# Attention: query slots of two rounds filled, and the first queries transposed, in the second layer's input stage; transposed keys kept in four banks

## What is computed

```python
h = _rmsnorm(x, attn_norm_w)
q = (h @ w_q).reshape(b, l, N_HEADS, HEAD_DIM)        # 16 heads of 16
k = (h @ w_k).reshape(b, l, N_KV_HEADS, HEAD_DIM)     # 4 key heads, each shared by 4 query heads
v = (h @ w_v).reshape(b, l, N_KV_HEADS, HEAD_DIM)
q = _apply_rope(q, cos, sin); k = _apply_rope(k, cos, sin)
logits = jnp.einsum('bqhd,bkhd->bhqk', q, k) * scale
attn = jax.nn.softmax(jnp.where(causal, logits, -inf), axis=-1)
ao = jnp.einsum('bhqk,bkhd->bqhd', attn, v)
```

## Time and profile before

| | us |
|---|---|
| median of 3 runs (lowest to highest) | 1553.54 (1552.95 to 1556.1) |
| span of the profiled execution | 1551.7 |
| input stage: first instruction, end of the last | 1259.48, 1309.46 |
| attention: first instruction, end of the last | 1309.98, 1426.76 |
| experts: first instruction | 1427.19 |
| PE busy / DVE busy / ACT busy / POOL busy over the span | 1401.1 / 1046.9 / 865.6 / 534.3 |

### The profile page before, as it was taken

One profiled execution on the slowest core, in us unless ns is written; L12 is line 12 of the kernel. 1 busy time (PEld: TensorE's weight loads), 2 busy tenths in 40 slices (PEclk: granted clock), 3 DMA queues, 4 the chain that ended last, 5 costly groups with the idle time before them and its releaser, 6 DMA issues. The chain is left out here.

```text
span 1551.7 us, 35674 instructions
## 1 busy us (share of the span) xinstructions
PE 1401.1 (90%) x13996; PEld 1045.2 (67%) x13996; DVE 1046.9 (67%) x2132; ACT 865.6 (56%) x1740; POOL 534.3 (34%) x562
## 2 busy tenths in 40 slices
PE   4569999999999999999999999999899977998998
PEld 3335767777776777777677777777578754555855
DVE  4887686877868687786858778686735544773344
ACT  5555656666666665666666666666355316676210
POOL 1872332342323233233323323333335446541100
PEclk9678999999999999999999999999989988999999
DMA  5112020201202021020102102110311130002100
GB/s 168 37 49 59 9 39 16 67 22 20 41 14 38 16 67 29 13 46 21 27 16 66 29 13 45 23 25 21 91 36 44 41 89 1 1 1 52 31 14 14
DMA packets 142486, 56.39 MB, mean 36 GB/s; under 512 B 109776, under 2 KB 134992, under 8 KB 142064
## 3 DMA queue, kind: packets, MB, share of 16 engines
q1 hardware_dynamic: 133424, 48.20, 13.4%
q10 hardware_dynamic: 8896, 5.91, 1.2%
HBM read 37.11 MB, written 16.97 MB: 35 GB/s over the span
## 5 line engine op out<-in xcount | busy, mean ns | idle before, releaser
L1153 POOL TENSOR_TENSOR og<-og,sz 128x256 f32<-128x256 f32 x128 | 93.3, 729 | 518.8 <-DVE og L1096 300.9
L690 PE MATMUL banks<-wz,xT 128*128 128x256 f32 x512 | 129.2, 397 | 13.8 <-DVE yacc L1116 13.8
L943 DVE SCALAR_TENSOR_TENSOR Yv<-banks,cwall,Yv 128x511 f32<-128x511 f32 (+2 forms) x192 | 130.3, 740 | 7.5 <-ACT Yv L783 7.4
L542 PE MATMUL banks<-wv,xT 128*128 128x512 f32 x256 | 121.5, 619 | 11.1 <-DVE Yv L943 9.6
L761 PE MATMUL banks<-wo,oT 128*128 128x256 f32 x512 | 123.8, 385 | 0.0
L542 PE MATMUL banks<-wqk,xT 128*128 128x512 f32 x256 | 121.7, 610 | 0.2 <-DVE Yk L943 0.2
L690 PEld LDWEIGHTS banks<-wz,xT 128*128 128x128 f32 x512 | 96.3, 196 | 36.6 <-issue 23.9
L930 ACT ACTIVATE junk<-og 128x512 f32<-128x512 f32 x64 | 40.6, 634 | 121.1 <-POOL og L1153 121.1
L1160 POOL TENSOR_TENSOR rn<-ss,c_half 128x4 f32<-128x4 f32 x64 | 64.5, 1007 | 122.0 <-DVE ss L1110 122.0
L761 PEld LDWEIGHTS banks<-wo,oT 128*128 128x128 f32 x512 | 93.6, 192 | 11.9 <-issue 0.7
L734 PE MATMUL banks<-V,A 128*128 128x128 f32 x512 | 85.8, 290 | 9.1 <-ACT V L910 9.1
(11 more groups left out here) (380 smaller groups left out, 3663.2 us busy)
## 6 DMA issues: line engine op xcount, KB each, us to landing
cm_d<-CM SPq DMA_DIRECT2D x32, 256.0 KB, 4.0
wqk<-in_L_attn_W_qkvz SPq DMA_DIRECT2D x8, 512.0 KB, 4.6
wv<-in_L_attn_W_qkvz SPq DMA_DIRECT2D x8, 512.0 KB, 4.2
wz<-in_L_attn_W_qkvz SPq DMA_DIRECT2D x16, 256.0 KB, 2.9
wo<-in_L_attn_W_out SPq DMA_DIRECT2D x16, 256.0 KB, 3.1
blk<-cm_d SPq DMA_DIRECT2D x128, 16.0 KB, 1.8
t_d<-tb SPq DMA_DIRECT2D x16, 128.0 KB, 1.7
Td<-t_d SPq DMA_DIRECT2D x128, 16.0 KB, 1.9
```

What stands on the lines that cost most here:

```text
L542: ins = pe.matmul(bank[b][:, :], xT[:, d, b * S + of_batch, :], w[:, d, :], start=(d == 0), stop=(d == KD - 1))
L690: ins = pe.matmul(bank[7][:, b * 256:(b + 1) * 256], xT[:, d, b * S + q, :], wz[:, d, :], start=(d == 0), stop=(d == KD - 1))
L943: v.scalar_tensor_tensor(y, bank[b][:, 0:T - j], conv_w(k, t)[:, 3 - j:4 - j], y, ALU.mult, ALU.add).then_inc(s["tap"].sem, 1)
L1153: pool.tensor_tensor(og[:, n, :, :], og[:, n, :, :], sz[q % 2][:, b, :].rearrange("p (h d) -> p h d", h=VR), ALU.mult).then_inc(s["osz"].s ...
```

## The change

In the input stage, the keys are transposed into four banks (0 to 3) with no wait between heads. ScalarE copies heads 0 and 1 out, VectorE heads 2 and 3. `ks` and `qs` are cleared in columns 96 to 127 only. After that GpSimd fills the slots of rounds 0 and 1 (12 copies), TensorE transposes round 0's slots into banks 4 and 5 (16 transposes, right behind the keys and ahead of products 14 and 15), and VectorE copies both halves out. In the attention, the slot copies of rounds 0 and 1 and F0 with its two ScalarE copies are gone, and so are the waits of round 0 on them. The due times, and so the order of all that is left, are the same.

```diff
@@ layer1_in
-    kT = am("kT", [P, KVH, TT, P], BF16)
+    kT, qT = am("kT", [P, KVH, TT, P], BF16), am("qTm0", [P, KVH, QT, P], BF16)
+    seats = lambda b, part: parts[:, part, b * QT:(b + 1) * QT, 0:D].rearrange("p t (g j e) -> p t g j e", g=KVH, j=REP)[:, :, :, 0, :]
@@ on_vector, at its end
+        for g in (2, 3):
+            v.wait_ge(*s["kTt"](g))
+            v.tensor_copy(kT[:, g, :, :], bank[g].bitcast(BF16).rearrange("p (t i) -> p t i", t=TT)).then_inc(s["kTe"].sem, 1)
+        for u in range(2):
+            v.wait_ge(*s["qTt"](u))
+            v.tensor_copy(qT[:, 2 * u:2 * u + 2, :, :], bank[4 + u].bitcast(BF16).rearrange("p (g t i) -> p g t i", g=2, t=QT)).then_inc(s["qTe"].sem, 1)
@@ on_scalar
-        for g in range(KVH):
+        for g in (0, 1):
             act.wait_ge(*s["kTt"](g))
-            act.copy(kT[:, g, :, :], bank[g % 2].bitcast(BF16).rearrange("p (t i) -> p t i", t=TT)).then_inc(s["kTe"].sem, 1)
+            act.copy(kT[:, g, :, :], bank[g].bitcast(BF16).rearrange("p (t i) -> p t i", t=TT)).then_inc(s["kTa"].sem, 1)
@@ on_tensor
         pe.wait_ge(*s["ks"]())
+        pe.wait_ge(*s["xTe"]())
+        pe.wait_ge(*s["vp"]())
         for g in range(KVH):
-            if g >= 2:
-                pe.wait_ge(*s["kTe"](g - 2))
             for t in range(TT):
-                ins = pe.transpose(bank[g % 2].bitcast(BF16)[:, t * P:(t + 1) * P], ks[:, t, g, :], c["identb"][:, :])
+                ins = pe.transpose(bank[g].bitcast(BF16)[:, t * P:(t + 1) * P], ks[:, t, g, :], c["identb"][:, :])
             ins.then_inc(s["kTt"].sem, 1)
+        pe.wait_ge(*s["slots"](4))
+        pe.wait_ge(*s["slot"](0))
+        for n in range(2):
+            for u in range(2 * QT):
+                ins = pe.transpose(bank[4 + n].bitcast(BF16)[:, u * P:(u + 1) * P], qs[:, u % QT, 2 * n + u // QT, :], c["identb"][:, :])
+            ins.then_inc(s["qTt"].sem, 1)
         for n in range(14, 16):
             pe_hidden(pe, n)
@@ on_gpsimd
-        pool.memset(ks[:, :, :, :], 0.0).then_inc(s["slots"].sem, 1)
+        pool.memset(ks[:, :, :, USED:P], 0.0).then_inc(s["slots"].sem, 1)
...
-        pool.memset(qs[:, :, :, :], 0.0).then_inc(s["slots"].sem, 1)
+        pool.memset(qs[:, :, :, USED:P], 0.0).then_inc(s["slots"].sem, 1)
+        for b in range(B):
+            for i, part in enumerate(Q_PARTS):
+                ins = pool.tensor_copy(qs[:, b * QT:(b + 1) * QT, :, i * HD:(i + 1) * HD], seats(b, part))
+            ins.then_inc(s["slot"].sem, 1)
@@ attention
-    first = lambda r: 2 * r - 1 if r else 0
-    second = lambda r: min(2 * r + 2, N + r)
+    first = lambda r: 2 * r - 2
+    second = lambda r: min(2 * r + 1, N + r - 1)
@@ pool_slots: the six copies stand under "if r >= 2"
@@ pe_first
-            pe.wait_ge(*s["qs"](0, r))
+            if r >= 2:
+                pe.wait_ge(*s["qs"](r - 2))
@@ pe_max
-            if t == 0:
+            if t == 0 and r:
                 pe.wait_ge(*s["turned"](2 * first(r) + g // 2))
@@ v_max
-        v.wait_ge(*s["turn"](2 * first(r) + 1))
+        if r:
+            v.wait_ge(*s["turn"](2 * first(r) + 1))
@@ rounds
-        in_order([(ROUND * r, f(engine, r)) for r in range(N) for f in kinds])
+        in_order([(ROUND * r, f(engine, r)) for r in range(N) for f in kinds if r or f not in (pe_first, act_first)])
```

More of the change, by code:

```diff
@@ L1520, in layer1_in @@
                      "xTt": TT, "xTe": TT, "qkv": TT, "ro": QT, "vp": TT, "rope": QT, "xhi": KD, "xlo": KD, "part": 3 * QT, "sub": 2 * QT, "slots": 5, "masks": 4, "ks": QT,
-                     "kTt": KVH, "kTe": KVH, "f1w": -2, "hid": 16, "h1": 16})
+                     "kTt": KVH, "kTa": 2, "kTe": 2, "slot": 2, "qTt": 2, "qTe": 2, "f1w": -2, "hid": 16, "h1": 16})
     xa, xn, xT = m["yacc"], m["xn"], m["xT"]
@@ L1731, in layer1_in @@
     stage_end(nc, s)
-    return {"parts": parts, "qs": qs, "kT": kT, "vp": vp, "by_query": by_query, "by_key": by_key}
+    return {"parts": parts, "qs": qs, "kT": kT, "qT": qT, "vp": vp, "by_query": by_query, "by_key": by_key}
 ROUND = 13.39
@@ L1748, in attention @@
     N = B * REP
-    s = signals(nc, {"qs": 1, "turn": 4 * N, "turned": 4 * N, "sc": 4 * QT, "mx": 4 * QT, "nm": 6, "e": 2 * QT, "ex": 2 * QT, "pv": QT, "oTe": 1, "oTt": 1, "rec": 1, "on": 1, "hhi": 1, "hlo": 1})
+    s = signals(nc, {"qs": N - 2, "turn": 4 * N - 2, "turned": 4 * N - 2, "sc": 4 * QT, "mx": 4 * QT, "nm": 6, "e": 2 * QT, "ex": 2 * QT, "pv": QT, "oTe": 1, "oTt": 1, "rec": 1, "on": 1, "hhi": 1, "hlo": 1})
     h1, (h_hi, h_lo) = m["h1"], m["h1_part"]
@@ L1753, in attention @@
     qs = [qs0[:, u * QT:(u + 1) * QT, :, :] for u in range(2)]
-    qT1, qT2 = ([am(f"{n}{u}", [P, KVH, QT, P], BF16) for u in range(2)] for n in ("qTm", "qTe"))
+    qT1, qT2 = [t_["qT"], am("qTm1", [P, KVH, QT, P], BF16)], [am(f"qTe{u}", [P, KVH, QT, P], BF16) for u in range(2)]
     mx, nm = ([am(f"{n}{u}", [P, QT, KVH]) for u in range(2)] for n in ("mx", "nm"))
@@ L1768, in pool_slots @@
             pool.wait_ge(*s["turn"](2 * second(r - 2) + 1))
-        for i, part in enumerate(Q_PARTS):
-            ins = pool.tensor_copy(qs[r % 2][:, :, :, i * HD:(i + 1) * HD], seats(j, b, part))
-        ins.then_inc(s["qs"].sem, 1)
+            for i, part in enumerate(Q_PARTS):
+                ins = pool.tensor_copy(qs[r % 2][:, :, :, i * HD:(i + 1) * HD], seats(j, b, part))
+            ins.then_inc(s["qs"].sem, 1)
         if r == 1:
```

## The result

The first comparison gave 1544.54 us (median of 7 runs, 1542.66 to 1554.25) against 1553.54 for the kernel before (7 runs, 1550.92 to 1556.29). Repeats of both kernels, further down, bring all runs to 1547.6 (31 runs, mean) against 1552.5 (94 runs of the same code, mean): 4.9 us, with a 95% interval of plus or minus 1.4. The forecast of the change was near, in part by luck (see the part on why the prediction was right and wrong); the forecast of the first comparison was not. Two questions follow: what the change does, and where the other 4 us came from.

What follows compares the result with a forecast made beforehand. TensorE paces later attention rounds, but nobody is busy around the barrier before them. First-round gain 4.5 us, less 0.2 for a later barrier, gives 4.3: 1553.5 - 4.3 = 1549.2 us, range 1546.5 to 1551.6.

Steps and rivals of the forecast that it cites:

- The strips give nothing: Input stage: clearing a quarter of `ks` finishes VectorE's normalizing some 2.7 us earlier, but gains nothing.
- cover: Input stage: a DMA at 1272.25, not VectorE, releases POOL's next instruction; without it up to 2.7 us would be gained.
- Product 14: End of the input stage on TensorE: starts at 1306.15 against 1306.64, 0.49 us earlier; at worst as before.
- The term of VectorE's copies: End of the input stage: four 1024-element copies out of PSUM at 1.23 us each, ending at 1309.7, last at the barrier.
- The rival: Input stage: VectorE's PSUM copies are fast, ScalarE ends last, barrier 0.5 us earlier; gain 5.0, time 1548.5; chance 0.20.
- X: Time engines leave the barrier before the attention (POOL's first instruction): from 1309.98 to 1310.2, 0.2 us later.
- Head start: Start of the attention: TensorE issues its first scores at X + 0.05 instead of X + 5.07.
- hold: Attention's first round: VectorE's `nm`, due at X + 10.2, is held until POOL's low part 1 ends at X + 11.36.
- S0: Attention step waiting for the `nm` chain, everything behind hangs on it: from X + 17.22 to X + 12.73, 4.5 us gained.
- near miss: Attention's first round: POOL's low part 1 ended 0.28 us ahead of `nm` before; now `nm` was to fall inside it.
- The clock: TensorE's clock around the attention's start: no net effect, 1.7 us either way; rival of another low stretch 1550.9, chance 0.16.
- my rivals: Whole kernel: fast copies 0.20, no hold 0.12, another low stretch 0.16, head start lost again 0.04, slower 0.05.

Runs made afterwards that it cites:

- The two experiments: Kernel after with GpSimd finishing before VectorE's chain begins (`b2_last`, 1543.82 us), and with GpSimd finishing later (`more_hold`, 1541.44 us).
- b2_last: Kernel after with the b2 sum moved to the end of GpSimd's attention queue; 1543.82 us, ratio 0.9943; repeated as b2_last_again: 1546.83 us, ratio 0.9967.
- again_after: Kernel after, unedited, run again beside the kernel before; 1548.68 us (12 runs), ratio 0.9984.
- after_third: Kernel after, unedited, third sample beside the kernel before; 1546.94 us (12 runs), ratio 0.9972.
- slots_only: Kernel after without the 16 early query transposes and their two copies, F0 back in the attention; 1547.38 us (10 runs), ratio 0.9960.
- more_hold: Kernel after with one more GpSimd copy of 128 x 256 elements behind the b2 sum, into an unread tile; 1541.44 us (one run).
- keys: Kernel before with only four banks for the keys, copies shared by ScalarE and VectorE; 1552.05 us (10 runs), ratio 1.0002.

## Why the prediction was right and wrong

**The strips give nothing**: right, cover and all.

**Input stage.** Product 14 starts 0.21, 0.50 and 0.55 earlier in the three profiles of after, where 0.49 was worked out. The term of VectorE's copies was mis-sized: 1.23 us each was taken from the rows that read PSUM; two take 1.29 together, and one takes 681 to 692 ns. The rival was right: the stage ends with ScalarE, and X comes 0.2 to 0.5 earlier, not 0.2 later. The rule of the Trainium skill (VectorE: DVE Perf Modes, The perf-mode tier table), that such a copy out of PSUM can run at up to two elements a cycle, agrees with the trace as far as it goes: 1024 elements in 681 ns are 0.67 ns an element, where the earlier trace rows had given 1.06. The rows I preferred were a reduction, and a copy with f32 output; neither was the operation in question.

**Head start and hold.** First score at X + 0.02 (X + 0.05 forecast), `nm` at X + 9.75 (X + 10.2), S0 at X + 12.58 in all three profiles (X + 12.73). The near miss of the earlier trace rows became the collision that was forecast, and longer, since `nm` came earlier: 1.60, 1.76 and 1.76 us. In the last two `nm` starts 0.15 sooner and lasts 0.16 longer, so the end does not move, as the prediction said. The Trainium skill (SBUF — State Buffer, Who interferes with whom) says that a VectorE `tensor_scalar` in a two-port mode and a GpSimd instruction share a pair of ports, and that whichever is issued first has it to its end. The two experiments agree as to the order and the length of the hold, even for 16 elements; that a shared pair of ports is behind it, no run here shows.

**The clock** was put at nil, with ends of 1.7 to either side. It costs 0.9 in the first profile of after (S0 to E 100.87 against 99.99) and 0.4 to 0.5 in the other two, since a stretch at the lower level now lies on dense work behind S0. `b2_last_again` has no such second stretch, and its S0 to E is 99.98, as before. Against that, in `again_after` and `after_third` the low stretch of the experts that answers to 1428.3 is missing, and E to the end takes 122.8 instead of 124.4. I do not count that for the change: its first profile and the versions `slots_only`, `b2_last`, `b2_last_again` and `more_hold` have 124.4 to 124.5. So the sum by measured terms is 4.64 (S0) + 0.19 (X) - 0.88 (clock) + 0.04 = 3.99 in the first profile, and 4.64 + 0.49 - 0.43 + 1.67 = 6.37 in the second; the forecast was 4.3, all runs together give 4.9. Up to E, where the change can act, the three profiles of after gain 3.9 to 4.7 on the first profile of before. That the forecast of 4.3 lies in there is in part luck: X was off by 0.4 to 0.7 us one way and the clock by 0.4 to 0.9 the other.

**The step that failed** is the last, from the sum to the number that a measurement shows: "1553.5 - 4.3 = 1549.2", with a range down to 1546.5, against a measured 1544.54. The prediction subtracted the gain from a median of three runs that lay some 3 us apart, put the variation of the first layer at nothing without giving a reason, and said that 0.2%, 3.1 us, can be told from no change. The runs showed in its place that the first layer, unedited, ends anywhere from 1249.68 to 1263.51. Single runs of one kernel spread with a standard deviation of 3.5 us (1542.85 to 1562.79 over 94 runs of before). Medians of a few runs move by one or two: the first median before was 1.1 above the mean of all, and the first after 3.1 below, and these two make up the 4 us between 9.0 and 4.9. None of my rivals was "the change does what I say and the comparison shows twice as much", and the range had no term for it. By an estimate from the 3.5 us of single runs, a difference between a median of seven and one of three is uncertain by some 5.6 us (95%), so that an honest range for the same theory would have run from about 1543.5 to 1555. The sign, faster, was right: by all runs together the gain is 4.9 us, 1.8 more than the 3.1 that were called the least to be told. The chances were also added up wrong: by the shares that the prediction names they give faster 0.74, same 0.24 and slower 0.03, not 0.76, 0.20 and 0.04.

## What to carry to other kernels

When a change pulls work ahead of a barrier, write down the queue of every engine behind it with start and end times, as a near miss of 0.3 us elsewhere turns into a collision; here moving one 4.5-us sum out of the way gave 2.0 us up to the experts, beside 3.9 to 4.7 for the change itself. Before a gain of a few us is read off two profiles, compare the part that was not edited: here 5.4 of 9.4 us lay there. And price an operation by a row of the same operation, output type included, or keep the whole gap in the range.

## What was not expected of the hardware

- PE pauses of 1.1 to 2.1 us within a run of 128 matmuls of 32 x 32, 1 to 6 of them in a profile. Which runs are cut changes from one execution to the next of the same build. All 41 pauses go with a block of instructions fetched as the run starts, and at or up to 4 us behind the end of 13 of them a stretch of 3.4 us at the lower clock level begins.
- With a microsecond less of waiting between the transposes of the keys, the low stretch behind the barrier was longer, not shorter, in the one profile taken: 17.1 us in `keys` against 13.65 before. The changed kernel's start of round 0, with no transposes and no pause for them, has 6.8 and 3.4 in its three profiles.
- VectorE's bf16 copy of 1024 elements out of PSUM takes 681 to 692 ns, as long as its f32 reduction of 512 (689).
